# Batch 0 of a two-layer kernel planned anew: x ahead of the mask, the mask in halves, the second bias turned before it is split

## The chip, the cores and the metric

One core of one Trainium2 chip. The metric is the device time of one execution in microseconds, the median of several runs.

## The reference

Eight batches of 256 rows and 1024 features go through two residual layers. In both the identity can be added to the weights.

```python
# layer 1: W0 (o, i), b0, a coefficient for each batch, a mask of 0 and 1 for each batch
x = x + (x @ W0.T + b0 + (x @ (2 * mask[b] - 1)) * coeff[b])
# layer 2: W1 (o, d), b1, and the adapter that ids[b] names (rank 16)
h = x @ A[ids[b]].T
x = x + (x @ W1.T + b1 + h @ B[ids[b]].T)
```

Input and output are float32; x is (8, 256, 1024), the mask (8, 1024, 1024) int32.

## The kernel before

**Precision.** Each float32 operand is split in two float32r parts, hi (a rounding copy, ScalarE) and lo (the rest, VectorE). A product is then three products: hi by hi, lo by hi, hi by lo.

**Tiles.** A chunk n is 128 output features of layer 1 in one batch: n = 8 b + c. make_w (VectorE) makes its weights from the mask and the turned W0, 128x1024; chunk_hi (ScalarE) and chunk_lo (VectorE) split them into whi and wlo. layer1(n, ks) on TensorE takes for each k of 128 inputs one product of 512 columns (whi against x hi and x lo, side by side) and one of 256 (wlo against x hi). The result is y: half_y (ScalarE) adds the bias b0, make_y (VectorE) adds the two halves, y_parts_hi and y_parts_lo split it to yhl. y of chunk c is the c-th input block of layer 2, which sums up in PSUM over the eight chunks. The adapter's h is computed from the same y (adapter_h), and b1 enters as two rows of bt in the closing products.

**Batch 0 against the rest.** From batch 1 on a regular loop runs. In batch 0 all weights have to be brought in and turned too: turn_unit (TensorE) transposes four 128x128 blocks of W0, W1, A, B or x into a PSUM bank; W0, W1, A and B each come in units of four blocks. GpSimd adds the identity to the diagonal block first (eye_w0, eye_w1), ScalarE copies W0 out (copy_w0), ScalarE and VectorE split the others (split_hi, split_lo). For batch 0 the program of every engine and of the DMA queue of SP is a list written out by hand; each engine takes its list in order. Chunks 0 and 1 are made and split in halves (half_make_w, half_chunk_hi, half_chunk_lo), x of batch 0 comes by rows (load_rows) and is turned on TensorE (first_rows_hi, first_rows_lo). x of batch 1 comes by load_x(1) into xraw and is turned on VectorE (turn_rows).

**Start.** SP issues W0 block 0, mask 0, rows 0 of x, b0, rows 1 of x, W0 block 1, mask 1, W1 block 0. TensorE runs products on zeros (idle_products, 512 columns each, in line L1056): five at first, two after the turn of the coefficients, three ahead of chunk 0. first_layer1 takes chunk 0: for k 0 to 3 the whi and the wlo product by turns, then W0's block 1 is turned, then k 4 to 7 in the same way, then the x lo products of k 0 to 7.

**The second bias.** load_b1 brings b1 into one partition (1x1024). bias_parts (GpSimd) makes b1hi and b1lo there; move_bias (SP) moves them to rows 80 and 81 of bt after clear_bt (GpSimd) has cleared bt, which waits for the turns of A. ScalarE's split_hi of B waits for both moves, for b1raw lies in the tile bhl that it writes. SP reads the eight adapter names into registers (read_names) in two groups of four.

**Waits that count below.** first_layer1 waits for x hi (x_hi), for whi and wlo's halves (first_hi, first_lo, w_hi, w_lo) and for x lo (x_lo). layer1(1) waits for first_lo of chunk 1, and its k 4 on for w_lo 2. The turn of W0 block 2 waits for y_made 1, since its bank is the one of chunk 0. first_layer2(c) waits for y_lo and the parts of W1's block c.

Of the kernel before, what the change touches and what calls it, by code (L numbers as in the profile page):

```python
# [7 lines left out]
I32 = mybir.dt.int32  # L8
# [8 lines left out]
def two_layer_kernel(nc, x, coeff, ids, mask, W0, b0, W1, b1, lora_a, lora_b, out):  # L17
# [46 lines left out]
    def parted(u):  # L64

        return sum(v[0] in ("w1", "a", "b") for v in units[:u + 1])

# [53 lines left out]
    with ExitStack() as ctx:  # L121
# [39 lines left out]
        b1raw = nc.alloc_sbuf_tensor_at("b1raw", [1, D], F32, offset=bhl_at)  # L161
        b1lo = nc.alloc_sbuf_tensor_at("b1lo", [1, D], F32R, offset=bhl_at)
        b1hi = nc.alloc_sbuf_tensor_at("b1hi", [1, D], F32R, offset=bhl_at + D * 4)
# [18 lines left out]
        rows_in = [sem(f"rows_in{st}") for st in range(ST)]  # L182
        mask_in = [sem(f"mask_in{s}") for s in range(MS)]
# [60 lines left out]
        def _(sp):  # L244
            def load_mask(n):
                b, c = divmod(n, KT)
                s = n % MS
                if n >= MS:
                    sp.wait_ge(w_lo, n - MS + 1)
                src = mask[b].rearrange("(p k) o -> p k o", k=KT)[:, :, c * P:(c + 1) * P]  # L250
                dst = wm[:, s, :].bitcast(I32).rearrange("p (k o) -> p k o", k=KT)
                sp.dma_start(dst, src).then_inc(mask_in[s], 16)
# [16 lines left out]
            def load_b1():  # L269
                sp.dma_start(b1raw[:, :], b1.rearrange("(e o) -> e o", e=1)).then_inc(b1_in, 16)  # L270
# [28 lines left out]
            def move_bias():  # L299
                sp.wait_ge(consts_set, 3)  # L300
                sp.wait_ge(bias_hi, 1)
                sp.dma_start(bt[80:81, :].bitcast(F32), b1hi[:, :].bitcast(F32)).then_inc(bias_moved, 16)
                sp.wait_ge(bias_lo, 1)
                sp.dma_start(bt[81:82, :].bitcast(F32), b1lo[:, :].bitcast(F32)).then_inc(bias_moved, 16)
# [75 lines left out]
            load_mask(11)  # L380
            load_mask(9)
            load_mask(10)
            load_bt(0)
# [16 lines left out]
        def _(pool):  # L400
# [60 lines left out]
            place_a(1)  # L461
            eye_w1(6)
            eye_w1(7)
            place_a(2)
# [6 lines left out]
        def _(act):  # L471
# [101 lines left out]
            first_rows_hi(0, 0)  # L573
            half_chunk_hi(0, 0)
            first_rows_hi(0, 1)
            first_rows_hi(1, 0)
            half_chunk_hi(0, 1)
            first_rows_hi(1, 1)
            copy_w0(1, 0)
            copy_w0(1, 1)  # L580
            half_y(0)
            half_chunk_hi(1, 0)
            half_chunk_hi(1, 1)
            split_hi("w1", 0, 0)
            split_hi("w1", 0, 1)
            copy_w0(2, 0)
            copy_w0(2, 1)
            y_parts_hi(0)
# [3 lines left out]
            chunk_hi(2)  # L592
            copy_w0(3, 0)
            y_parts_hi(1)
# [8 lines left out]
            copy_w0(4, 1)  # L603
            split_hi("w1", 3, 0)
            y_parts_hi(2)
# [4 lines left out]
            copy_w0(5, 1)  # L610
            split_hi("b", 0, 0)
            chunk_hi(5)
            y_parts_hi(3)
            split_hi("w1", 4, 0)
            split_hi("w1", 4, 1)
            half_y(4)
            copy_w0(6, 0)
            copy_w0(6, 1)
            y_parts_hi(4)
            split_hi("b", 0, 1)  # L620
            split_hi("w1", 5, 0)
            chunk_hi(6)
            half_y(5)
            split_hi("w1", 5, 1)
            copy_w0(7, 0)
            copy_w0(7, 1)
            y_parts_hi(5)
            split_hi("w1", 6, 0)
            chunk_hi(7)
            split_hi("w1", 6, 1)  # L630
            half_y(6)
            rows_hi(1, 1)
            y_parts_hi(6)
            split_hi("w1", 7, 0)
            chunk_hi(8)
            rows_hi(1, 0)
            split_hi("w1", 7, 1)
            half_y(7)
# [30 lines left out]
        def _(dve):  # L669
# [29 lines left out]
            def make_w(n):  # L699
                b, c = divmod(n, KT)  # L700
                dve.wait_ge(mask_in[n % MS], 16 * (n // MS + 1))
# [14 lines left out]
            def half_make_w(n, g):  # L716

                dve.wait_ge(mask_in[n], 16)
# [93 lines left out]
            split_lo("w1", 1, 0)  # L812
            make_y(1)
            split_lo("w1", 1, 1)
# [6 lines left out]
            split_lo("a", 0, 1)  # L821
            chunk_lo(3)
            make_y(2)
            make_w(4)
            split_lo("w1", 3, 0)
            split_lo("w1", 3, 1)
            y_parts_lo(2)
# [419 lines left out]
```

## Time and profile before

| | us |
|---|---|
| median of 3 runs | 407.26 (406.19 to 407.48) |
| the profiled execution | 407.4 |
| its span, first to last instruction | 405.6 |
| TensorE busy | 397.5 (98%) |
| VectorE busy | 293.0 (72%) |
| ScalarE busy | 182.8 (45%) |
| GpSimd busy | 26.7 (7%) |
| DMA, mean | 156 GB/s |

PE is TensorE (PEld its weight loads), DVE VectorE, ACT ScalarE, POOL GpSimd, SP the engine that issues the loads (SPq its DMA issues). A matmul's duration includes its way through the array, so matmuls overlap; from start to start is what one costs in a row. Times are from the start of the span.

### The profile page before, as it was taken

The numbers are of one execution on the slowest core, as the hardware profiler recorded it, in microseconds if no ns is written. First come the engines' busy times: TensorE is split into PE (matmuls) and PEld (weight loads), VectorE is DVE, ScalarE is ACT, GpSimd is POOL, SyncE is SP. The second block draws the span as 40 slices with busy tenths as digits, with TensorE's granted clock in tenths as the row PEclk, the third lists the DMA queues.
The fourth block names the chain that finished last, engine by engine and source line by source line (L and its number), as shares of the span: only waits on it lengthen the run. The fifth ranks groups of instructions, "written<-read, shape, count | busy, mean of one in ns | idle before, by whom it ended". The sixth has DMA issues, their size and how long they took to land.

```text
span 405.6 us, 6148 instructions
## 1 busy us (share of the span) xinstructions
PE 397.5 (98%) x2362; PEld 365.9 (90%) x2362; DVE 293.0 (72%) x375; ACT 182.8 (45%) x289; POOL 26.7 (7%) x43
## 2 busy tenths in 40 slices
PE   7989999999999999999999999999999999999996
PEld 5878888899999999999999999999999999999995
DVE  1797799766977598677887679675987688775523
ACT  2666656443444344343445344354444444353322
POOL 1253121000001000010001000010001000000000
PEclk9999999999999999999999999999999999999999
DMA  8999993659532893159532893249732792346002
GB/s 260 305 251 281 283 231 99 146 156 253 149 103 105 182 221 103 53 152 251 156 105 73 190 228 94 79 127 211 192 104 72 201 242 77 103 133 166 0 2 103
DMA packets 93488, 63.33 MB, mean 156 GB/s; under 512 B 3595, under 2 KB 90643, under 8 KB 93460
## 3 DMA queue, kind: packets, MB, share of 16 engines
q1 hardware_dynamic: 93298, 62.77, 59.7%
q8 instruction: 19, 0.31, 0.3%
q10 hardware_dynamic: 162, 0.18, 0.1%
q14 instruction: 9, 0.07, 0.1%
HBM read 51.39 MB, written 8.39 MB: 147 GB/s over the span
## 4 chain that ended last, share of the span: by engine, by line
PE 95%; DVE 2%; DMA 2%; ACT 0%; SPq 0%; issue 0%
PE ps L951 29%; PE ps L953 15%; PE ps L1022 13%; PE ps L1024 13%; PE ps L1023 13%; PE ps L924 4%; PE ps L1045 2%; PE ps L1000 2%; DMA xrows<-in_x_dram 2%; PE ps L1002 2%; PE ps L1001 2%; DVE yhl L752 1%; PE ps L985 0%; DVE wlo L712 0%; PE ps L1056 0%; DVE h_rows L767 0%
## 5 line engine op out<-in xcount | busy, mean ns | idle before, releaser
L951 PE MATMUL ps<-xhl,whi 128*128 128x512 f32 x504 | 180.3, 396 | 0.0
L953 PE MATMUL ps<-xhl,wlo 128*128 128x256 f32 x504 | 140.9, 280 | 0.0
L951 PEld LDWEIGHTS ps<-xhl,whi 128*128 128x128 f32 x504 | 94.5, 188 | 19.2
L1024 PE MATMUL ps<-w1hi,yhl 128*128 128x344 f32 (+1 forms) x336 | 107.8, 321 | 0.0
L1022 PE MATMUL ps<-w1hi,yhl 128*128 128x344 f32 (+1 forms) x336 | 107.6, 320 | 0.0
L1023 PE MATMUL ps<-w1lo,yhl 128*128 128x344 f32 (+1 forms) x336 | 107.6, 320 | 0.0
L953 PEld LDWEIGHTS ps<-xhl,wlo 128*128 128x128 f32 x504 | 95.0, 189 | 0.5
L712 DVE SCALAR_TENSOR_TENSOR wlo<-wm,cs_minus,whi 128x1024 fp32r<-128x1024 f32 x62 | 79.7, 1285 | 20.6 <-ACT whi L492 20.6
L492 ACT ACTIVATE whi<-wm,cs_minus 128x1024 fp32r<-128x1024 f32 x62 | 71.5, 1153 | 38.1 <-DVE wm L705 38.1
L705 DVE SCALAR_TENSOR_TENSOR wm<-wm,cs_twice,w0t 128x1024 f32<-128x1024 int32 x62 | 79.7, 1286 | 1.1 <-ACT w0t L475 1.1
L748 DVE TENSOR_TENSOR ysum<-ps,ysum 128x256 f32<-128x256 f32 x64 | 27.1, 424 | 59.9 <-ACT ysum L532 59.9
L532 ACT ACTIVATE ysum<-ps,b0col 128x256 f32<-128x256 f32 x64 | 30.3, 473 | 87.4 <-PE ps L953 85.8
L1022 PEld LDWEIGHTS ps<-w1hi,yhl 128*128 128x128 f32 x336 | 63.1, 188 | 3.0 <-DVE yhl L752 0.3
L1023 PEld LDWEIGHTS ps<-w1lo,yhl 128*128 128x128 f32 x336 | 63.2, 188 | 0.0
L1024 PEld LDWEIGHTS ps<-w1hi,yhl 128*128 128x128 f32 x336 | 63.1, 188 | 0.0
L539 ACT ACTIVATE yhl<-ysum 128x256 fp32r<-128x256 f32 x64 | 26.8, 419 | 27.6 <-DVE ysum L748 27.6
L682 DVE STREAM_TRANSPOSE xt<-xraw 128x1024 f32<-128x1024 f32 x14 | 31.2, 2228 | 3.7 <-DMA xraw<-in_x_dram 3.7
L752 DVE TENSOR_TENSOR yhl<-ysum,yhl 128x256 fp32r<-128x256 f32 x64 | 30.0, 469 | 1.2 <-ACT yhl L539 1.2
L517 ACT ACTIVATE xhl<-xt 128x1024 fp32r<-128x1024 f32 x14 | 14.9, 1062 | 21.6 <-DVE xt L682 21.6
L434 POOL CAST w1hi<-at 128x128 fp32r<-128x128 f32 x7 | 6.1, 872 | 223.9 <-PE ps L1024 223.9
L688 DVE TENSOR_TENSOR xhl<-xt,xhl 128x1024 fp32r<-128x1024 f32 x14 | 17.1, 1219 | 0.0
L1000 PE MATMUL ps<-w1hi,yhl 128*128 128x512 f32 x32 | 13.4, 420 | 1.4 <-DVE yhl L752 1.4
(78 smaller groups left out, 241.2 us busy)
## 6 DMA issues: line engine op xcount, KB each, us to landing
wm<-in_mask_Bx4096x_ik_dram SPq DMA_DIRECT2D x64, 512.0 KB, 5.2
xraw<-in_x_dram SPq DMA_DIRECT2D x28, 256.0 KB, 6.3
w0raw<-in_L_cond_W_dram SPq DMA_DIRECT2D x8, 512.0 KB, 6.2
w1raw<-_L_cond_base_weight_dram SPq DMA_DIRECT2D x8, 512.0 KB, 7.3
out_dram<-zst SPq DMA_DIRECT2D x18, 172.0 KB, 2.0
bt<-bhl SPq DMA_DIRECT2D x48, 64.0 KB, 2.4
out_dram<-zst SPq DMA_DIRECT2D x8, 164.0 KB, 2.0
out_dram<-zst SPq DMA_DIRECT2D x7, 176.0 KB, 2.0
```

The costliest lines, as they stand in the source:

```text
L492: nc.scalar.activation(whi[:, n % WS, :, :], wm[:, n % MS, :].rearrange("p (k o) -> p k o", k=KT), ACT.Identity, bias=cs_minus[:, b:b + 1] ...
L532: nc.scalar.activation(ysum[:, n % 2, :], ps[:, l1_bank(n), S:2 * S], ACT.Identity, bias=b0col[:, n % KT:n % KT + 1]).then_inc(y_half, 1)
L682: nc.vector.transpose(xt[:, :, :].rearrange("p t (n q) -> p n t q", q=Q), xraw[:, :, :].rearrange("p n (i k) -> p n k i", k=KT)[:, :, g * ...
L705: nc.vector.scalar_tensor_tensor(chunk, chunk.bitcast(I32), cs_twice[:, b:b + 1], w0t[:, c, :, :].rearrange("p k o -> p (k o)"), ALU.mult, ...
L712: nc.vector.scalar_tensor_tensor(wlo[:, s, :, :], wm[:, n % MS, :].rearrange("p (k o) -> p k o", k=KT), cs_minus[:, b:b + 1], whi[:, s, :, ...
L748: nc.vector.tensor_tensor(row, ps[:, l1_bank(n), 0:S], row, ALU.add).then_inc(y_made, 1)
L752: nc.vector.tensor_tensor(yhl[:, n % 2, S:2 * S], ysum[:, n % 2, :], yhl[:, n % 2, 0:S].bitcast(F32), ALU.subtract).then_inc(y_lo, 1)
L951: nc.tensor.matmul(ps[:, bank, :], whi[:, s, k, :], xhl[:, b % 2, k, :], start=(k == 0), stop=False, skip_group_check=True)
L953: op = nc.tensor.matmul(ps[:, bank, 0:S], wlo[:, s, k, :], xhl[:, b % 2, k, 0:S], start=False, stop=(k == KT - 1), skip_group_check=True)
L1022: nc.tensor.matmul(dst, hi, w1hi[:, c, cols], start=(c == 0), stop=False, skip_group_check=True)
L1023: nc.tensor.matmul(dst, hi, w1lo[:, c, cols], start=False, stop=False, skip_group_check=True)
L1024: op = nc.tensor.matmul(dst, lo, w1hi[:, c, cols], start=False, stop=(c == KT - 1), skip_group_check=True)
```

## The change

No arithmetic is added or left out.

- **Order of the first loads.** W0 block 0, rows 0 of x, b0, the first half of mask 0, rows 1 of x, the second half of mask 0, W0 block 1, mask 1. The mask halves are two DMAs of 256 KB with a semaphore each (first_mask_in), in the same pieces of 512 bytes; half_make_w(0, g) waits for its half.
- **Chunk 0's products in three parts for each half g:** part 0 whi by x hi, part 1 wlo by x hi, part 2 whi by x lo, with a wait of their own each. Order on TensorE: (0,0), (0,1), the turns of W0 block 1, (1,1), (1,0), (0,2), (1,2).
- **Zeros.** Seven at the start, two ahead of the turn of the coefficients (which so comes later), none ahead of chunk 0: nine instead of ten.
- **The second bias.** b1 is loaded as 128x8 (pieces of 32 bytes), split there as 128x8, and the two moves gather the 128 pieces into a row of bt. bias_parts comes after clear_bt and eye_w1(3) on GpSimd; its load comes after that of A's pieces 4 to 7 and mask 3.
- **Batch 0 planned anew** on SP, GpSimd, ScalarE, VectorE and TensorE; the loop from chunk 8 on is as before.

```diff
             load_w0(0)
-            load_mask(0)
             load_rows(0)
             load_b0()
+            load_first_mask(0)
             load_rows(1)
+            load_first_mask(1)
             load_w0(1)
             load_mask(1)
             sp.wait_ge(ids_in, 16)
             load_w1(0)
+            load_w0(2)
             names = read_names(range(0, 4))
-            load_w0(2)
-            load_b1()
-            names += read_names(range(4, 8))
             load_w1(1)
             load_mask(2)
             load_w0(3)
-            load_b(range(0, 2))
+            names += read_names(range(4, 8))
             load_w1(2)
             load_a(range(4, 6))
+            load_a(range(6, 8))
             load_mask(3)
-            load_a(range(6, 8))
+            load_b1()
             load_a(range(0, 2))
             load_a(range(2, 4))
+            load_b(range(0, 2))
             load_w0(4)
             load_w1(3)
             load_mask(4)
+            load_w0(5)
             load_b(range(2, 4))
-            load_w0(5)
-            load_w1(4)
             load_b(range(4, 6))
             load_b(range(6, 8))
+            load_w1(4)
             move_bias()
             load_mask(5)
+            load_w1(5)
             load_w0(6)
             load_w0(7)
             load_mask(6)
-            load_w1(5)
             load_x(1)
...
             load_w1(7)
-            load_mask(11)
+            load_bt(0)
             load_mask(9)
             load_mask(10)
-            load_bt(0)
+            load_mask(11)
```

```diff
+            def load_first_mask(g):
+
+                src = mask[0].rearrange("(p k) o -> p k o", k=KT)[:, g * TG:(g + 1) * TG, 0:P]
+                dst = wm[:, 0, g * HALF:(g + 1) * HALF].bitcast(I32).rearrange("p (k o) -> p k o", k=TG)
+                sp.dma_start(dst, src).then_inc(first_mask_in[g], 16)
...
-                sp.dma_start(b1raw[:, :], b1.rearrange("(e o) -> e o", e=1)).then_inc(b1_in, 16)
+                sp.dma_start(b1raw[:, :], b1.rearrange("(p k) -> p k", k=KT)).then_inc(b1_in, 16)
...
-                sp.dma_start(bt[80:81, :].bitcast(F32), b1hi[:, :].bitcast(F32)).then_inc(bias_moved, 16)
+                sp.dma_start(bt[80:81, :].bitcast(F32).rearrange("e (p k) -> e p k", k=KT), b1hi[:, :].bitcast(F32)).then_inc(bias_moved, 16)
```

GpSimd's and TensorE's lists, the latter to the turns of W0 block 5; ScalarE's and VectorE's follow the same order of chunks.

```diff
             eye_w1(2)
+            eye_w0(4)
+            clear_bt()
+            eye_w1(3)
             bias_parts()
-            eye_w0(4)
-            eye_w1(3)
-            clear_bt()
             eye_w0(5)
             sort_b()
+            place_a(1)
             eye_w1(4)
...
-            idle_products(5)
+            idle_products(7)
             pe.wait_ge(ident_set, 2)
             turn_unit("w0", 0, 0)
             turn_unit("w0", 0, 1)
-            pe.wait_ge(coeff_spread, 1)
-            nc.tensor.transpose(ps[:, L1B, 0:NB], cs_rows[:, :], ident[0:NB, 0:NB]).then_inc(coeff_turned, 1)
             idle_products(2)
+            turn_coeff()
             turn_unit("x", 0, 0)
             turn_unit("x", 0, 1)
-            turn_b0()
             turn_unit("x", 1, 0)
             turn_unit("x", 1, 1)
-            idle_products(3)
-            first_layer1(range(0, 4), False)
+            turn_b0()
+            first_layer1(0, 0)
+            first_layer1(0, 1)
             turn_unit("w0", 1, 0)
             turn_unit("w0", 1, 1)
-            first_layer1(range(4, 8), False)
-            first_layer1(range(0, 4), True)
-            first_layer1(range(4, 8), True)
+            first_layer1(1, 1)
+            first_layer1(1, 0)
+            first_layer1(0, 2)
+            first_layer1(1, 2)
             turn_unit("w1", 0, 0)
             turn_unit("w1", 0, 1)
+            layer1(1, range(0, 2))
             turn_unit("w0", 2, 0)
+            layer1(1, range(2, 4))
             turn_unit("w0", 2, 1)
-            layer1(1, range(0, 2))
-            layer1(1, range(2, 4))
             layer1(1, range(4, 6))
             turn_unit("w1", 1, 0)
             turn_unit("w1", 1, 1)
             layer1(1, range(6, 8))
             first_layer2(0, 0, 0)
+            first_layer2(0, 1, 0)
             first_layer2(0, 0, 1)
             turn_unit("w0", 3, 0)
-            first_layer2(0, 1, 0)
+            first_layer2(0, 1, 1)
             turn_unit("w0", 3, 1)
-            first_layer2(0, 1, 1)
             turn_unit("w1", 2, 0)
+            layer1(2, range(0, 2))
             turn_unit("w1", 2, 1)
+            layer1(2, range(2, 4))
+            layer1(2, range(4, 6))
+            turn_unit("a", 0, 0)
+            turn_unit("a", 0, 1)
+            layer1(2, range(6, 8))
             first_layer2(1, 0, 0)
             first_layer2(1, 1, 0)
-            layer1(2, range(0, 2))
-            turn_unit("a", 0, 0)
-            turn_unit("a", 0, 1)
             first_layer2(1, 0, 1)
-            layer1(2, range(2, 4))
-            layer1(2, range(4, 6))
-            layer1(2, range(6, 8))
             turn_unit("w0", 4, 0)
-            adapter_h(0)
             turn_unit("w0", 4, 1)
             first_layer2(1, 1, 1)
+            adapter_h(0)
+            adapter_h(1)
             turn_unit("w1", 3, 0)
             turn_unit("w1", 3, 1)
             layer1(3, range(0, 2))
             layer1(3, range(2, 4))
             layer1(3, range(4, 6))
             turn_unit("w0", 5, 0)
+            adapter_h(2)
             layer1(3, range(6, 8))
             turn_unit("w0", 5, 1)
```

VectorE's list of chunk 0 and 1:

```diff
             half_make_w(0, 0)
+            first_rows_lo(0, 0)
             half_make_w(0, 1)
-            first_rows_lo(0, 0)
             half_chunk_lo(0, 0)
             first_rows_lo(1, 0)
             half_chunk_lo(0, 1)
+            move_b0()
             first_rows_lo(0, 1)
-            move_b0()
             first_rows_lo(1, 1)
             half_make_w(1, 0)
             half_make_w(1, 1)
+            half_chunk_lo(1, 0)
             make_y(0)
-            half_chunk_lo(1, 0)
+            split_lo("w1", 0, 0)
             half_chunk_lo(1, 1)
-            split_lo("w1", 0, 0)
+            y_parts_lo(0)
             split_lo("w1", 0, 1)
-            y_parts_lo(0)
             make_w(2)
```

## Rows read from the trace of the kernel before

**Rows 1.** Page, part 1: busy time and share of each engine.

```profile
PE 397.5 (98%) x2362; PEld 365.9 (90%) x2362; DVE 293.0 (72%) x375; ACT 182.8 (45%) x289; POOL 26.7 (7%) x43
```

**Rows 2.** Stretches: from:to length, busy of each engine, granted clock, DMA share, GB/s.

```profile
23.30:29.50 6.20, 4.80 (x30) 3.96 (x28) 6.16 (x7) 4.31 (x8) 4.66 (x3) 1.00 1.05 227
29.50:80.60 51.10, 51.05 (x293) 43.96 (x294) 42.36 (x49) 29.47 (x48) 9.98 (x15) 1.00 0.84 212
80.60:405.60 325.00, 321.31 (x1935) 300.89 (x1933) 232.17 (x301) 137.25 (x213) 6.91 (x11) 1.00 0.53 137
```

**Rows 3.** Waits, whole span: who <- for whom: us, times, longest.

```profile
PE ps L1000 <- DVE yhl L752: 1.4, 1, 1.4
...
PEld ps L924 <- DVE ysum L748: 0.4, 1, 0.4
```

**Rows 4.** Timeline to 20 us, TensorE: start, duration, line, op [idle before].

```profile
1.32 2.50 PE L1056 MATMUL ps<-zeros 128*128 128x512 f32 x5 [1.32 <-POOL zeros L437]
...
4.96 1.94 PE L924 MATMUL ps<-ident,w0raw 128*128 128x128 f32 x8 [1.14 <-POOL w0raw L405]
...
8.60 1.97 PE L924 MATMUL ps<-ident,xrows 128*128 128x128 f32 x8 [0.34 <-DMA xrows<-in_x_dram]
...
12.33 1.50 PE L1056 MATMUL ps<-zeros 128*128 128x512 f32 x3
...
13.67 0.28 PE L973 MATMUL ps<-xhl,whi 128*128 128x256 f32 x1
...
17.44 1.04 PE L924 MATMUL ps<-ident,w1raw 128*128 128x128 f32 x8
...
18.63 1.16 PE L924 MATMUL ps<-ident,w0raw 128*128 128x128 f32 x8
...
19.57 0.50 PE L951 MATMUL ps<-xhl,whi 128*128 128x512 f32 x1
```

**Rows 5.** Timeline to 20 us, ScalarE and VectorE.

```profile
9.82 0.60 ACT L522 ACTIVATE xhl<-ps 128x512 fp32r<-128x512 f32 x1 [2.28 <-PE ps L924]
...
10.32 0.71 ACT L502 ACTIVATE whi<-wm,cs_minus 128x512 fp32r<-128x512 f32 x1
...
15.97 1.62 DVE L721 SCALAR_TENSOR_TENSOR wm<-wm,cs_twice,w0t 128x512 f32<-128x512 int32 x2 [0.85 <-ACT w0t L475]
```

**Rows 6.** Timeline: the split of the second bias, and yhl's low part twice.

```profile
25.88 3.22 POOL L416 TENSOR_TENSOR b1lo<-b1raw,b1hi 1x1024 fp32r<-1x1024 f32 x1
...
26.81 2.58 DVE L752 TENSOR_TENSOR yhl<-ysum,yhl 128x256 fp32r<-128x256 f32 x1
...
47.04 0.41 DVE L752 TENSOR_TENSOR yhl<-ysum,yhl 128x256 fp32r<-128x256 f32 x1
```

**Rows 7.** Landings of mask 0, A's last, x(1)'s last piece; starts of users.

```profile
DMA to landing us min/median/max: 5.5/5.5/5.5
...
L292 SPq DMA_DIRECT2D araw<-in_L_cond_lora_A_w_dram x1: 315/315/315, 25.2 to 25.2; - x1
...
DMA to landing us min/median/max: 5.2/5.2/5.2
...
31.72 1.04 PE L924 MATMUL ps<-ident,araw 128*128 128x128 f32 x8
...
33.80 0.46 POOL L410 TENSOR_TENSOR w1raw<-w1raw,ident 128x128 f32<-128x128 f32 x1 [1.33 <-DMA w1raw<-_L_cond_base_weight_dram]
...
37.20 1.03 PE L924 MATMUL ps<-ident,w1raw 128*128 128x128 f32 x8
...
L261 SPq DMA_DIRECT2D xraw<-in_x_dram x1: 1113/1113/1113, 45.4 to 45.4; - x1
...
DMA to landing us min/median/max: 9.6/9.6/9.6
...
57.42 2.24 DVE L682 STREAM_TRANSPOSE xt<-xraw 128x1024 f32<-128x1024 f32 x1
...
67.36 0.48 PE L951 MATMUL ps<-xhl,whi 128*128 128x512 f32 x1
```

More of the change, by code:

```diff
@@ L182, in two_layer_kernel @@
         rows_in = [sem(f"rows_in{st}") for st in range(ST)]
+        first_mask_in = [sem(f"first_mask_in{g}") for g in range(2)]
         mask_in = [sem(f"mask_in{s}") for s in range(MS)]
@@ L460, in _ @@
             eye_w1(5)
-            place_a(1)
+            place_a(2)
             eye_w1(6)
             eye_w1(7)
-            place_a(2)
             pool.wait_ge(z_done, sums_before(1))
@@ L821, in _ @@
             split_lo("a", 0, 1)
+            make_y(2)
             chunk_lo(3)
-            make_y(2)
             make_w(4)
             split_lo("w1", 3, 0)
+            y_parts_lo(2)
             split_lo("w1", 3, 1)
-            y_parts_lo(2)
             chunk_lo(4)
@@ L834, in _ @@
             split_lo("w1", 4, 1)
+            chunk_lo(5)
             make_y(4)
-            chunk_lo(5)
             make_w(6)
-            y_parts_lo(4)
             split_lo("b", 0, 1)
             split_lo("w1", 5, 0)
+            y_parts_lo(4)
             chunk_lo(6)
+            split_lo("w1", 5, 1)
             make_y(5)
-            split_lo("w1", 5, 1)
             turn_rows(1, 1)
+            y_parts_lo(5)
             make_w(7)
-            y_parts_lo(5)
+            rows_lo(1, 1)
             split_lo("w1", 6, 0)
+            chunk_lo(7)
+            make_y(6)
+            split_lo("w1", 6, 1)
             make_w(8)
-            split_lo("w1", 6, 1)
-            make_y(6)
-            chunk_lo(7)
-            rows_lo(1, 1)
             y_parts_lo(6)
@@ L956, in layer1, with first_layer1 @@
                     op.then_inc(l1_done, 1)
-            def first_layer1(ks, low):
-                if ks[0] == 0 and not low:
-                    pe.wait_ge(first_lo, 1)
-                for k in ks:
-                    if k == TG and not low:
-                        pe.wait_ge(w_lo, 1)
-                    if k % TG == 0 and low:
-                        pe.wait_ge(x_lo, first_lo_split(ST - 1, k // TG))
-                    elif k % TG == 0:
-                        pe.wait_ge(x_hi, first_split(ST - 1, k // TG))
-                    if low:
-                        op = nc.tensor.matmul(ps[:, l1_bank(0), S:], whi[:, 0, k, :], xhl[:, 0, k, S:],
-                                              start=(k == 0), stop=(k == KT - 1), skip_group_check=True)
-                    else:
-                        nc.tensor.matmul(ps[:, l1_bank(0), 0:S], whi[:, 0, k, :], xhl[:, 0, k, 0:S],
-                                         start=(k == 0), stop=False, skip_group_check=True)
-                        nc.tensor.matmul(ps[:, l1_bank(0), 0:S], wlo[:, 0, k, :], xhl[:, 0, k, 0:S],
-                                         start=False, stop=(k == KT - 1), skip_group_check=True)
-                if low and ks[-1] == KT - 1:
+            def first_layer1(g, part):
+                if part == 0 and g == 0:
+                    pe.wait_ge(first_hi, 1)
+                elif part == 0:
+                    pe.wait_ge(w_hi, 1)
+                elif part == 1 and g == 0:
+                    pe.wait_ge(first_lo, 1)
+                elif part == 1:
+                    pe.wait_ge(w_lo, 1)
+                if part == 2:
+                    pe.wait_ge(x_lo, first_lo_split(ST - 1, g))
+                else:
+                    pe.wait_ge(x_hi, first_split(ST - 1, g))
+                weights = wlo if part == 1 else whi
+                cols = slice(S, 2 * S) if part == 2 else slice(0, S)
+                for k in range(g * TG, (g + 1) * TG):
+                    op = nc.tensor.matmul(ps[:, l1_bank(0), cols], weights[:, 0, k, :], xhl[:, 0, k, cols],
+                                          start=(k == 0 and part != 1), stop=(k == KT - 1 and part > 0), skip_group_check=True)
+                if g == 1 and part == 2:
                     op.then_inc(l1_done, 1)
@@ L1051, in turn_b0, with turn_coeff @@
                 nc.tensor.transpose(ps[:, L1B, 0:KT], b0row[:, :], ident[0:KT, 0:KT]).then_inc(b0_turned, 1)
+            def turn_coeff():
+                pe.wait_ge(coeff_spread, 1)
+                nc.tensor.transpose(ps[:, L1B, 0:NB], cs_rows[:, :], ident[0:NB, 0:NB]).then_inc(coeff_turned, 1)
             def idle_products(count):
@@ L1126, in _ @@
             first_layer2(2, 1, 0)
             layer1(4, range(4, 6))
+            turn_unit("w1", 4, 1)
+            first_layer2(2, 1, 1)
             layer1(4, range(6, 8))
[L1129 removed]
             turn_unit("w0", 6, 0)
+            adapter_h(3)
             turn_unit("w0", 6, 1)
             first_layer2(3, 0, 0)
[L1133 removed]
+            first_layer2(3, 1, 0)
             turn_unit("b", 0, 1)
[L1135 removed]
+            layer1(5, range(0, 2))
```

88 lines of the change are left out of this document (43 added, 45 removed).

## The prediction

> **What bounds the kernel now.** I read the page's shares first: TensorE is busy 397.5 of 405.6 us [rows 1], so time can only come from its work, its waits, or its speed. The stretches say where the 8 us without it lie: from 80.6 us on it is busy 321.3 of 325.0, from 29.5 to 80.6 it is busy 51.05 of 51.10, and from 23.3 to 29.5 only 4.80 of 6.20 [rows 2]. The list of waits names the largest one after the start: 1.4 us for VectorE's yhl, the low part of y of chunk 1, then 0.4 us for ysum [rows 3]. The timeline of the first 20 us gives the rest: 1.3 us before the first instruction, 1.1 us before the first transposes (while GpSimd adds ident to w0(0)), 0.3 us for x, and fillers (the products on zeros) that count as busy but do nothing for the output: five at 1.32, three at 12.33 [rows 4].
>
> The same rows show a second loss that no share shows. Eight transposes take 1.97 us at 8.60 and 1.04 us at 17.44; three fillers of 512 columns take 1.50 us at 12.33, as much as 1.2 GHz needs, while the products of chunk 0 start at 13.67 at the rate of 2.4 GHz [rows 4]. The granted clock reads 1.00 throughout [rows 2], so here it is the durations that tell the level: lower until about 13.6 us, upper afterwards. From 30 us on the kernel is a full queue on TensorE. Hence the sum: whatever makes TensorE reach its state at 30 us earlier is kept to the end, if no other engine or load becomes late.
>
> **Part 1: x ahead of the mask, mask in halves, products in three parts.** Now rows 0 of x land at 8.60 (TensorE waits for them), after chunk 0's mask, issued at 1.2 and landed 5.5 later, at 6.7 [rows 4, 7]. Both are 512 KB, so in the new order x should land at about 6.7, the first half of the mask 0.9 later (half of the 1.9 between the two landings), at 7.6, rows 1 near 9.2 and the second half near 10. Bounds for a half: nothing later than the whole mask's place in the present queue, and 2 us later if two issues cost more than one.
> TensorE: the transposes of w0(0) still wait for GpSimd and start at 4.96; the seven fillers end before (two more are 0.9 us, beside a wait of 1.1). Then come two fillers (0.9) and the turn of the coefficients, which is put behind them, so x starts at 7.75 instead of 8.60. x(0) takes 1.9 at the lower level, x(1) starts at about 9.6.
> ScalarE: its first x part comes 1.2 us after the transposes start (9.82 against 8.60) [rows 4, 5], so now at 9.0. Four x parts of 0.6 and the half of whi of 0.7 [rows 5], at the pace at which the units arrive, put the third x part's end at 11.6. VectorE has the first half of wlo ready at 11.8 (0.8, as one of the two halves of w that take 1.62 [rows 5]).
> So the first products start at 11.7 instead of 13.67. Four products of 256 columns are 0.85 us at the lower level and 0.47 at the upper: the first two parts fill 11.7 to 13.4, w0(1)'s eight transposes 13.4 to 14.2 (0.8 start to start), two more parts go to 15.3. The part with wlo's second half needs 13.5 on VectorE, and does not wait. The last part needs x's last low part, VectorE 14.9. It ends at 16.2, against 17.44 when the w1 transposes begin behind it [rows 4]: 1.2 us.
> What is late next is VectorE. It makes w of chunk 1 from 14.9 instead of 15.97, where today it waits for the w0 copy [rows 5]. Two halves of 0.8 and wlo's half, again near 0.75, give 17.2. TensorE has done w1(0)'s transposes at 17.0, so it waits 0.2. Today it starts chunk 1 at 19.57, behind w0(2)'s transposes of 18.63 [rows 4], which wait 0.4 for ysum [rows 3]; in the new order w0(2) comes inside chunk 1. The like place is therefore 18.63, and the shift there is 1.4. The second half of wlo(1) is ready at about 19.55, when TensorE arrives at 19.6: an even race. Splitting w0(2) costs one or two restarts of 0.1. I carry a shift of 1.25 through chunk 1, bounds 0.6 (VectorE 0.6 late at the even race) and 1.7 (no wait, clock up earlier).
>
> **Part 2: the second bias.** Today GpSimd splits it as 1x1024: 3.22 us from 25.88, and beside it VectorE's yhl takes 2.58 us instead of 0.41 [rows 6]; TensorE's 1.4 us wait ends with exactly that instruction [rows 3, 6]. As 128x8 the two steps work on 8 elements of a partition. The trace has no such step on GpSimd; above it is bounded by the 0.46 us of a 128x128 step [rows 7], below by nothing. I take 0.2 each. Without the stall yhl would end 2.2 us earlier, before TensorE asks, and its order is changed too (chunk 2 of layer 1 goes ahead of layer 2 of chunk 1), so the whole 1.4 goes; what is late next is wlo of chunk 2, about 25 on VectorE against 26 on TensorE. The step also moves behind clear_bt and w1(3). SP stands in move_bias until it is done, with mask 5, w1(5), w0(6), w0(7), mask 6 and x(1) queued behind in SP's program. It arrives there near 35, and w1(3) is added to ident on GpSimd at 33.80 today [rows 7], so the bias is split by 34.7: no new wait, up to 1 us on SP if w1(3) lands late. The moves and the load are now 128 pieces of 32 bytes. Nothing in the trace prices these; ScalarE needs them only for the first b unit.
>
> **Part 3: the new plan of batch 0.** No TensorE work is added or removed but one filler (nine instead of ten) and a few restarts; there is nothing to gain where TensorE is busy 51.05 of 51.10 [rows 2], so it can only lose. The loads set this. The DMA engines are full from 23.3 to 29.5 (share 1.05) and at 0.84 over the next 51 us [rows 2], so the loads do not come earlier, while TensorE comes 2.6 us earlier. Adapter a: the last piece is issued at 25.2 and lands at 30.4, TensorE turns it at 31.72 [rows 7], and would now, 2.65 us earlier with seven pieces of layers 1 and 2 behind chunk 1 as before, want it at about 29.0. It gets ahead of b and the bias, issued some 1.6 us earlier, landing at 28.8: I charge 0.2, bounds 0 and 1.3. w1(3): turned at 37.20 today [rows 7], 2.65 earlier and behind one adapter product more it is wanted at about 34.8; it is ready at 34.3 (33.80 + 0.46), behind the same bytes: 0 to 0.5. x(1): the last piece lands at 45.4 + 9.6 = 55.0, VectorE turns it at 57.42 [rows 7], and now wants it at 54.8; VectorE may stand 0.2 to 0.5, with y_parts_lo(5), make_w(7) and chunk_lo(7) queued behind it. chunk_lo(7) ends some 6.7 us after that turn begins (2.24 for the turn, the other steps 4.5 by their kind), and TensorE, which takes chunk 7 of layer 1 at 67.36 today [rows 7], wants it at about 64.8: three us of cover. load_bt(0) goes ahead of masks 9 to 11; six small issues, in a stretch with slack. place_a(1) is put ahead of w1(4) on GpSimd; w1(4) then has about 1 us of cover left.
>
> **Sum.** 1.25 + 1.4 - 0.2 for a, +0.1 for the filler and small waits = 2.55 us. The profiled execution took 407.4 us with a span of 405.6, so 1.8 lie outside it; it becomes 403.05 + 1.8 = 404.85. It stands 0.14 above the median of the runs, 407.26, so the forecast is 404.7.
>
> **Rivals.**
> (a) One gain is swallowed: VectorE or the landing of a, w1(3) or b takes about half. For it: the even race at 19.6 and three covers under 1 us. Against it: VectorE loses 2.2 us of stall at 27, and TensorE's order puts long pieces of layer 1 ahead of what was late. Lower ends of the parts, 0.6 + 1.4 - 0.8: 1.2 us, so about 406.0.
> (b) The clock, which ends on the slower side. Place: 11 to 20 us. Today three fillers, 1.5 us without a pause, stand just ahead of the rise at 13.6 [rows 4]; they are gone. Price: each us for which the lower level lasts longer costs 0.5 us of TensorE, less what VectorE covers. If the rise comes at 17, at the end of chunk 0's products, 1.4 us are lost: 406.2. The forecast's gain is used up when the lower level lasts until 18.8, and the kernel is slower by over 0.3% (1.2 us more) from a rise at 21.2, say 408.8. Against it: the fillers are replaced by real products at 11.7, as long as the fillers were, and TensorE has fewer pauses ahead of them.
> The Trainium skill speaks for this rival: "TensorE: Matmul & The Clock Gate", Part 4: PE-mode transpose, says that transposes do not count as TensorE activity for the clock as products do. By that rule the x transposes do nothing for the clock and the removed fillers did; the trace agrees as far as 16 transposes of x from 8.60 to 12.3 ran wholly at the lower level, and the rise came only after fillers, but it does not tell the one cause from the other.
> (c) More is gained: the rise comes ahead of the x(1) transposes, the race at 19.6 is won, and a lands in time: 1.7 + 1.4 + 0.1 = 3.2, so 404.1, or a little less, 403.9.
>
> **How the numbers follow.** Forecast 0.50 (404.0 to 405.5); (a) 0.22; (b) 0.13 near 406.2 and 0.07 slower; (c) 0.08. A measurement of this kernel can tell about 0.3% from no change, which is 1.2 us: faster ends at 406.0, slower begins at 408.5. The forecast and (c) are faster whole, (a) for half, (b) for a quarter of its 0.13: 0.50 + 0.08 + 0.11 + 0.03, 0.72; same 0.11 of (a) and 0.10 of (b), 0.21; slower 0.07. The range leaves out the slow end of (b) and the best of (c): 403.6 to 406.6.
>
> **What would show it.** Right, step by step: x's transposes start near 7.8; the first product of chunk 0 at 11.7 and the w1 transposes behind the last one at 16.2 to 16.6; chunk 1 near 17.3; transposes at 0.1 us each from 13.6 at the latest; GpSimd's bias steps under 0.5 us and no yhl over 0.6 us; no TensorE wait over 0.3 us between 20 and 80; the last product of batch 0 2.5 us earlier than now. Wrong: a TensorE wait on a, w1(3) or wlo(1) (a), products of 256 columns at 0.21 us apart after 14 us (b), or a hole on VectorE at x(1) that reaches TensorE.

## The result

The changed kernel takes 404.77 us, the median of 7 runs (404.1 to 406.26), against 407.26 before (406.17 to 409.27): ratio 0.9946, interval 0.9925 to 0.9968. The forecast was 404.7. A second set of runs, on another chip, gave 0.9966 (0.9946 to 0.9987). So it is faster by 1.4 to 2.2 us. The profiled execution, 406.26 us with a span of 404.5, is the longest of the seven: what follows explains an execution 1.5 us slower than the median, whose span is only 1.1 us shorter than that of the trace of before.

Page of the changed kernel, parts 1 to 3 (busy, packets):

```profile
PE 394.7 (98%) x2361; PEld 363.7 (90%) x2361; DVE 288.9 (71%) x375; ACT 183.5 (45%) x289; POOL 21.5 (5%) x43
...
DMA packets 93870, 63.33 MB, mean 157 GB/s; under 512 B 3978, under 2 KB 91026, under 8 KB 93842
```

The same bytes and, but for one filler, the same products; TensorE's busy time is 2.8 us less than in [rows 1], VectorE's 4.1 and GpSimd's 5.2. Timeline of the changed kernel, TensorE:

```profile
1.33 3.35 PE L1075 MATMUL ps<-zeros 128*128 128x512 f32 x7 [1.33 <-POOL zeros L449]
4.78 1.38 PE L939 MATMUL ps<-ident,w0raw 128*128 128x128 f32 x8
...
6.71 1.16 PE L939 MATMUL ps<-ident,xrows 128*128 128x128 f32 x8
...
8.35 1.16 PE L939 MATMUL ps<-ident,xrows 128*128 128x128 f32 x8 [0.48 <-DMA xrows<-in_x_dram]
...
9.85 0.71 PE L990 MATMUL ps<-xhl,whi 128*128 128x256 f32 x4 [0.19 <-ACT xhl L534]
...
14.84 1.07 PE L939 MATMUL ps<-ident,w1raw 128*128 128x128 f32 x8 [0.70 <-POOL w1raw L422]
...
15.66 0.48 PE L966 MATMUL ps<-xhl,whi 128*128 128x512 f32 x1
...
29.34 0.84 PE L939 MATMUL ps<-ident,araw 128*128 128x128 f32 x6 [1.51 <-DMA araw<-in_L_cond_lora_A_w_dram]
...
79.31 0.39 PE L1051 MATMUL ps<-bt,ht 128*128 128x512 f32 x1
```

Against [rows 4]: eight x transposes take 1.16 us instead of 1.97, chunk 0's products start at 9.85 instead of 13.67, chunk 1 at 15.66 instead of 19.57 (3.0 earlier than the like place, 18.63). A is turned at 29.34 against 31.72 [rows 7]: of 3.0 us in hand, and the wait of 1.4 us for yhl gone as well, 2.4 are left. At the closing product of batch 0 (80.50 in the first trace of before) 1.2 are left. From there to the end it is 325.2 us in the changed kernel (404.5 less 79.31) and 325.1 in the one before (405.6 less 80.50). So all of the change, gain and loss, lies ahead of 80 us, and in this execution more than half of what the head (all that lies ahead of chunk 1) gained was given back by then. TensorE's waits say where:

```profile
PE ps L939 <- DMA araw<-in_L_cond_lora_A_w_dram: 1.5, 1, 1.5
...
PE ps L939 <- POOL w1raw L422: 1.2, 2, 0.7
PE ps L939 <- DVE bhl L687: 1.2, 1, 1.2
PE ps L939 <- DMA xrows<-in_x_dram: 0.5, 1, 0.5
```

The wait for yhl of [rows 3] is gone; in its place stand A, W1's blocks (0.7 ahead of chunk 1, 0.5 at 24.65), and bhl, the split of B. That last one is a load too, one step removed. VectorE stood for mask 6 with B's split queued behind it in its list (timeline of the changed kernel, VectorE):

```profile
51.28 1.28 DVE L717 SCALAR_TENSOR_TENSOR wm<-wm,cs_twice,w0t 128x1024 f32<-128x1024 int32 x1 [2.43 <-DMA wm<-in_mask_Bx4096x_ik_dram]
52.48 1.08 DVE L687 TENSOR_TENSOR bhl<-ps,bhl 128x512 fp32r<-128x512 f32 x1
```

Mask 6 was issued at 39.1 and landed 12.1 us later. The DMA engines are full all the while (stretches of the changed kernel, as in [rows 2]):

```profile
20.00:27.50 7.50, 6.98 (x43) 6.04 (x42) 4.49 (x8) 4.67 (x8) 0.92 (x2) 1.00 1.14 219
...
30.00:52.00 22.00, 22.00 (x137) 19.36 (x136) 14.19 (x18) 14.85 (x24) 8.63 (x15) 1.00 1.12 279
```

The DMA share is over 1 in both, but the bytes are not at one rate, 219 and 279 GB/s.

### The profile page after: what moved, and what is told of

It is laid out like the page before. It is cut to its first block, busy times and chain, and to the rows that moved or that the text cites. A ratio compares the mean times of both kernels' runs of the same rounds, so it can differ in the third digit from the quotient of the medians.

```text
span 404.5 us, 6149 instructions
## 1 busy us (share of the span) xinstructions
PE 394.7 (98%) x2361; PEld 363.7 (90%) x2361; DVE 288.9 (71%) x375; ACT 183.5 (45%) x289; POOL 21.5 (5%) x43
## 4 chain that ended last, share of the span: by engine, by line
PE 87%; SPq 5%; DMA 4%; DVE 2%; issue 1%; ACT 0%
PE ps L966 27%; PE ps L968 14%; PE ps L1037 13%; PE ps L1039 13%; PE ps L1038 13%; DMA wm<-in_mask_Bx4096x_ik_dram 3%; PE ps L1060 2%; DMA araw<-in_L_cond_lora_A_w_dram 1%; PE ps L939 1%; SPq L287 1%; PE ps L1017 1%; PE ps L1015 1%; PE ps L1016 1%; SPq L298 1%; SPq L303 1%
## 5 line engine op out<-in xcount | busy, mean ns | idle before, releaser
L551 ACT ACTIVATE yhl<-ysum 128x256 fp32r<-128x256 f32 x64 | 26.8, 419 | 27.9 <-DVE ysum L763 27.5
L767 DVE TENSOR_TENSOR yhl<-ysum,yhl 128x256 fp32r<-128x256 f32 x64 | 27.5, 429 | 1.0 <-ACT yhl L551 1.0
L529 ACT ACTIVATE xhl<-xt 128x1024 fp32r<-128x1024 f32 x14 | 14.9, 1064 | 20.1 <-DVE xt L694 20.1
L687 DVE TENSOR_TENSOR w1lo<-ps,w1hi 128x512 fp32r<-128x512 f32 x16 | 10.8, 687 | 5.0 <-ACT w1hi L497 4.9
```

What stands on the lines that cost most here:

```text
L767: nc.vector.tensor_tensor(yhl[:, n % 2, S:2 * S], ysum[:, n % 2, :], yhl[:, n % 2, 0:S].bitcast(F32), ALU.subtract).then_inc(y_lo, 1)
```

## The experiments

Two theories. **Loads:** the loads keep the DMA engines full until about 52 us and do not come earlier, so whatever lets TensorE arrive earlier is given back at the next load. **Sum:** the parts add up. Beside them stood a question on the clock: do the seven fillers bring the upper level early, or is it chance? Every kernel was timed against the kernel before on the same chip; the ratios are to that one. There were four sets, on which the kernel before had these medians: 407.26 with the changed kernel (after); 406.88 with b_narrow, a_wide, a_fill5 and b_fill7; 406.59 with b_head, a_mask_first and a_again; 406.51 with a_early, a_mask6, a_both and both_mask_first. Medians of different sets are therefore compared by their ratios.

| kernel | x | chunk 0 | chunk 1 | A | closing | median us | ratio (95%) |
|---|---|---|---|---|---|---|---|
| before | 8.60 | 13.67 | 19.57 | 31.72 | 80.50 | 407.26 | |
| b_again | 8.70 | 13.15 | 19.05 | 30.09 | 79.53 | | |
| b_fill7 | 8.62 | 13.78 | 19.90 | 32.12 | 80.95 | 406.32 | 0.9988 (0.9968, 1.0008) |
| b_narrow | 8.32 | 11.87 | 17.82 | 32.12 | 81.00 | 406.26 | 0.9983 (0.9963, 1.0002) |
| b_head | 6.49 | 10.06 | 17.33 | 29.78 | 79.21 | 406.04 | 0.9980 (0.9963, 0.9997) |
| after | 6.71 | 9.85 | 15.66 | 29.34 | 79.31 | 404.77 | 0.9946 (0.9925, 0.9968) |
| a_again | 6.50 | 10.35 | 16.20 | 29.14 | 78.12 | 405.08 | 0.9966 (0.9946, 0.9987) |
| a_fill5 | 7.59 | 10.73 | 16.05 | 28.67 | 77.48 | 404.88 | 0.9952 (0.9932, 0.9972) |
| a_mask_first | 7.94 | 11.08 | 16.67 | 29.32 | 79.72 | 405.53 | 0.9980 (0.9961, 0.9999) |
| a_wide | 6.39 | 9.75 | 15.60 | 28.45 | 79.68 | 406.59 | 1.0001 (0.9974, 1.0028) |
| a_early | 6.81 | 9.95 | 15.74 | 28.31 | 78.34 | 404.78 | 0.9956 (0.9937, 0.9975) |
| a_mask6 | 6.67 | 9.87 | 15.94 | 29.50 | 78.77 | 405.74 | 0.9982 (0.9964, 1.0000) |
| a_both | 6.55 | 9.76 | 15.83 | 28.07 | 79.94 | 405.26 | 0.9966 (0.9948, 0.9984) |
| both_mask_first | 8.98 | 12.36 | 17.79 | 29.12 | 78.66 | 405.74 | 0.9977 (0.9951, 1.0003) |

The columns x to closing are starts on TensorE in the one trace of each kernel, from its timeline: the first transposes of x, the first products of chunk 0 and of chunk 1, the transposes of A, the first closing product. Executions of one kernel differ by more than most of these kernels do (the changed one took 403.58 to 406.97 us over both sets, the one before 404.71 to 409.73), so a single trace shows which waits there are, not what they cost in the median.

### The second bias, alone and undone

b_narrow is the kernel before with these lines of the change and no other; a_wide is the changed kernel with them undone:

```diff
-        b1raw = nc.alloc_sbuf_tensor_at("b1raw", [1, D], F32, offset=bhl_at)
-        b1lo = nc.alloc_sbuf_tensor_at("b1lo", [1, D], F32R, offset=bhl_at)
-        b1hi = nc.alloc_sbuf_tensor_at("b1hi", [1, D], F32R, offset=bhl_at + D * 4)
+        b1raw = nc.alloc_sbuf_tensor_at("b1raw", [P, KT], F32, offset=bhl_at)
+        b1hi = nc.alloc_sbuf_tensor_at("b1hi", [P, KT], F32R, offset=bhl_at + KT * 4)
+        b1lo = nc.alloc_sbuf_tensor_at("b1lo", [P, KT], F32R, offset=bhl_at + 2 * KT * 4)
```

> The kernel before with the second bias as 128x8 (load, split, moves) and nothing else. Both theories: the 1.4 us wait of TensorE for yhl at 29.5 us goes, GpSimd's two bias steps take under 1.5 us together instead of 4.3, no yhl step on VectorE is over 0.7 us. If the parts of the change simply add up, the time is 1.4 us lower than the kernel before (ratio about 0.9966). If the loads are the next bound, TensorE comes 1.4 us earlier to the transposes of A, whose last piece lands 1.3 us before TensorE wants it today, so 1.2 to 1.4 us are still gained.

> The changed kernel with the second bias as 1x1024 again (load, split, moves), all orders as in the changed kernel. If the parts add up: slower than the changed kernel by 1.4 us or more, since GpSimd's 4 us stall VectorE again. If loads bind the changed kernel up to 54 us (its trace shows TensorE standing 1.5 us for A and 1.2 us behind a late mask): the stall falls on time that is idle anyway, the time is within 0.6 us of the changed kernel.

b_narrow's ratio is 0.7 us lower, half of what was expected, with an interval from 1.5 us lower to 0.1 higher, so that no gain at all is not ruled out. The bias steps are short (0.44 and 0.21 us), no yhl stalls, but TensorE now waits for W0's block 3:

```profile
PE ps L924 <- POOL w0raw L405: 3.1, 2, 2.0
```

(The other 1.1 us is the wait at the start.) That block was issued at 14.6 and landed 9.4 us later; in the trace of before it was issued at 14.9 and landed 6.7 later. So the load itself came 2.3 us later here. Whether that is scatter or the 128 small pieces of b1, issued 3.7 us ahead of it, was not tried.

The pause has a second price in this trace. Its stretches from 20 us on (length, busy, then granted clock, DMA share, GB/s at the end):

```profile
20.00:24.00 4.00, 3.14 (x20) 2.44 (x18) 3.63 (x6) 2.60 (x4) 0.00 (x0) 1.00 0.98 257
24.00:27.00 3.00, 1.86 (x11) 1.76 (x12) 0.88 (x2) 0.90 (x2) 1.46 (x3) 0.90 0.75 188
27.00:31.00 4.00, 4.00 (x18) 3.42 (x17) 1.05 (x3) 1.79 (x3) 0.48 (x2) 0.65 0.86 263
```

The clock is granted 0.90 and 0.65 of full behind the pause of 2.0 us, 1.2 GHz for a part of each. The head start that this trace had at chunk 1 (17.82 against 19.57) was gone at A (32.12, later than before).

a_wide costs 1.4 to 2.2 us against the changed kernel (1.0001 against 0.9966 and 0.9946). In its own set stands a_fill5, the changed kernel but for two fillers, with 0.9952 (0.9932 to 0.9972) against 0.9974 to 1.0028 for a_wide, so the loads did not hide it. In its place behind W1's block 3 the wide step falls on w of chunk 4 (timeline of a_wide, GpSimd, VectorE, TensorE):

```profile
33.03 3.24 POOL L428 TENSOR_TENSOR b1lo<-b1raw,b1hi 1x1024 fp32r<-1x1024 f32 x1
...
33.97 4.78 DVE L717 SCALAR_TENSOR_TENSOR wm<-wm,cs_twice,w0t 128x1024 f32<-128x1024 int32 x1
...
36.24 0.45 POOL L417 TENSOR_TENSOR w0raw<-w0raw,ident 128x128 f32<-128x128 f32 x1
...
36.64 1.03 POOL L436 COPY bsort<-braw 128x1024 f32<-128x1024 f32 x1
...
39.41 0.72 PE L939 MATMUL ps<-ident,w0raw 128*128 128x128 f32 x4 [2.07 <-DVE w1lo L687]
```

VectorE's step ended only at 38.75, 2.5 us after the bias step: two more steps of GpSimd, the last two of its rows shown, ran beside it with no gap (in the changed kernel they start at 35.73 and 37.30, apart). So here the loads theory was wrong and the sum nearer: the stall comes behind A's wait, with its own place on VectorE.

### The fillers and the clock

a_fill5 is the changed kernel with idle_products(5) for idle_products(7), b_fill7 the kernel before with 7 for 5; b_again is the kernel before once more, a_again the changed one.

> The changed kernel with five fillers at the start instead of seven. Theory clock: the two more fillers are what brings the upper level before w0(0)'s transposes end; with five, x's transposes take 0.21 us each, the products of chunk 0 start 1 to 2 us later than 9.85, and as the loads bind later stretches the time rises by 0 to 0.8 us only. Rival: the early rise comes from the order of x or by chance; then x's transposes stay at 0.1 us each and nothing changes.

> The kernel before with seven fillers at the start instead of five, nothing else. Theory clock: the upper level comes before 8.6 us, x's transposes take 0.1 us each, and chunk 0's products start 0.8 to 1.5 us earlier than 13.67, the time falls by 0.7 to 1.5 us. Rival: x's transposes stay at 0.21 us, the rise stays near 13.5 us and the time is the same within 0.3 us.

> The kernel before unchanged, for a second trace. If the moment of the rise is the program's doing, it is near 13.5 us again, behind the three fillers. If it is free, it lies elsewhere (the kernel with seven fillers at the start had it near 14.3, the one with the narrow bias near 9.4).

> The changed kernel unchanged, for a second trace and more times. If the moment at which the clock rises is the program's doing, x's transposes take 0.1 us each again and the rise is near 5.4 us. If it is free, it lies elsewhere between 4 and 9 us, and the waits for A and for W1's block 5 (1.5 and 1.2 us in the first trace) shift by as much as TensorE comes later.

Neither experiment on the fillers shows an effect on the time: a_fill5 0.9952 beside 0.9946 and 0.9966 for the changed kernel, b_fill7 0.9988 with 1 in its interval. Timeline of b_fill7, then of b_head, which run the same TensorE program up to the end of W0's first transposes:

```profile
1.32 3.35 PE L1056 MATMUL ps<-zeros 128*128 128x512 f32 x7 [1.32 <-POOL zeros L437]
4.81 1.94 PE L924 MATMUL ps<-ident,w0raw 128*128 128x128 f32 x8
```

```profile
1.32 3.35 PE L1075 MATMUL ps<-zeros 128*128 128x512 f32 x7 [1.32 <-POOL zeros L449]
4.81 1.13 PE L939 MATMUL ps<-ident,w0raw 128*128 128x128 f32 x8
```

The same work with the same starts: 1.94 us at the lower level in the one, 1.13 at the upper in the other. The moment of the rise is not the program's alone. Yet it is not all chance either: in the four traces with the old head the x transposes begin at the lower level, in the eight with x first at the upper one, with five fillers too (a_fill5: sixteen in 2.03 us). What in the new head does it the runs do not tell, but they narrow it down. It is not the order of the loads: in a_mask_first and both_mask_first the mask comes ahead of x again, and x's transposes still begin at the upper level (at 7.94 and 8.98). It is not the number of fillers, by a_fill5 and b_fill7. And it is not pauses ahead of x: a_fill5 stands 0.88 us ahead of W0's transposes and is at the upper level by 7.59, b_fill7 has no pause up to 8.10 and stays at the lower one until about 14. Nor does it take the three fillers of the old head, behind which the rise came in the trace of before: in b_narrow, with the same program on TensorE, it came at about 9.4, amid x's transposes and ahead of the three fillers:

```profile
8.32 1.57 PE L924 MATMUL ps<-ident,xrows 128*128 128x128 f32 x8
...
9.98 1.16 PE L924 MATMUL ps<-ident,xrows 128*128 128x128 f32 x8
```

b_again had no wait for yhl at all: the bias step fell there on w of chunk 3 (1.90 us on VectorE), and TensorE waited 0.4 for A instead. Its one execution took 407.21 us, within the range of the other runs of this kernel.

### The head alone, and undone

b_head is the kernel before with the new order of the first six loads, the mask halves, the three parts, the fillers and the lists of chunk 0. a_mask_first is the changed kernel with this:

```diff
+            load_first_mask(0)
+            load_first_mask(1)
             load_rows(0)
             load_b0()
-            load_first_mask(0)
             load_rows(1)
-            load_first_mask(1)
```

> The kernel before with the new head only: x ahead of the mask, the mask in halves, chunk 0 in three parts, seven and two fillers, the lists of chunk 0 as in the changed kernel; the second bias wide and the plan behind chunk 0 as before. If the sum of the prediction holds, chunk 0's products end 1.2 us earlier at the same clock, the 1.4 us wait for yhl stays, and the time falls by 1.2 to 1.4 us (ratio about 0.997). If the head's gain in the changed kernel was the early clock alone, the time is within 0.5 us of before and depends on when the transposes change from 0.21 to 0.1 us each.

> The changed kernel with both halves of mask 0 loaded ahead of x, all else as changed. If the order of x carries the head's gain: x lands near 8.6 us again, chunk 0's products start 1.3 to 2 us later than 9.85, and the time rises by 0.8 to 1.5 us. If the loads of A, W1 and the masks bind later anyway, the late head is absorbed by those waits and the time stays within 0.5 us of the changed kernel.

b_head gains 0.8 us (0.1 to 1.5), less than the 1.2 to 1.4 expected, though its products start 3.6 us earlier. Its waits:

```profile
PE ps L939 <- POOL w1raw L422: 2.6, 3, 1.5
...
PE ps L939 <- DMA araw<-in_L_cond_lora_A_w_dram: 0.2, 1, 0.2
```

W1's block 2 is late now, 1.5 us. The 1.4 us wait for yhl, which was expected to stay since the second bias is still wide, is not in the list: as in b_again the wide step fell on w of chunk 3 (1.89 us). By the ratios the head alone and the bias alone gain 0.8 and 0.7 us, 1.5 together; the whole change gains 1.4 in one set and 2.2 in the other. So in the final time the parts do add up within the noise, each at less than was expected of it, and the noise is too large to say whether the rest of the plan adds anything. a_mask_first starts chunk 1 1.0 us later than the changed kernel and turns A at 29.32 against 29.34: the wait for A shrank from 1.5 to 1.0, the rest went in others. Its median is 0.5 us above that of the changed kernel in the same set (by the ratios 0.6 and 1.4 us above the two sets), and the intervals overlap; whether x first is worth anything in the final time was not settled.

### Taking the loads' waits away

a_early loads A's pieces 0 to 3 ahead of mask 3 and b1, a_mask6 loads mask 6 ahead of W0's block 7, a_both does both, both_mask_first adds the edit of a_mask_first.

```diff
             load_a(range(6, 8))
+            load_a(range(0, 2))
+            load_a(range(2, 4))
             load_mask(3)
             load_b1()
-            load_a(range(0, 2))
-            load_a(range(2, 4))
...
             load_w0(6)
-            load_w0(7)
             load_mask(6)
+            load_w0(7)
```

> The changed kernel with all eight pieces of A loaded ahead of mask 3 and b1. If A's landing pins TensorE at about 29 us (it turns A at 28.5 to 29.8 in six traces whose chunk 1 starts anywhere from 15.6 to 17.3), the wait for A of 1.0 to 1.5 us shrinks below 0.4 and A is turned near 28; mask 3 lands 0.8 us later, which VectorE has cover for. Time 0.5 to 1.2 us lower than the changed kernel. Rival, the queue only changes place: the wait moves to mask 3 or W1 block 3 and the time is the same within 0.3 us.

> The changed kernel with mask 6 loaded ahead of W0's block 7. If the 1.2 us wait of TensorE at 52.4 us comes from mask 6 (VectorE stood 2.4 us for it with B's split queued behind), VectorE's wait falls under 1 us, TensorE's under 0.2, and the time falls by up to 1.2 us where the wait occurs; the second trace of the changed kernel had only 0.2 there, so 0.3 to 0.8 us in the median. Rival: the wait is chance, time the same within 0.3 us.

> Both of these. If both waits are the loads' and independent: 1.0 to 1.8 us lower than the changed kernel, ratio to the kernel before 0.990 to 0.993. If taking away one exposes the other (the loads as a whole are the bound until 54 us), no more than the better of the two alone.

> As a_both, with both halves of mask 0 loaded ahead of x. With the changed plan alone this made chunk 1 start 1.0 us later and A was turned at the same moment. If A's landing no longer pins TensorE, the later head now shows: 0.5 to 1.0 us slower than a_both. If the loads still bind, within 0.3 us of a_both.

Each wait that was aimed at goes, and another one stays or grows. In a_early no wait for A is listed and A is turned at 28.31; the waits are now these:

```profile
PE ps L939 <- POOL w1raw L422: 1.7, 2, 1.1
...
PE ps L939 <- DVE bhl L687: 1.1, 1, 1.1
```

Its ratio of 0.9956 lies between the two sets of the changed kernel: the gain of 0.5 to 1.2 us did not come. In a_mask6 VectorE makes w of chunk 6 at 49.11 without a wait, the one for bhl is not in the list, and A's is 1.9. Its ratio of 0.9982 is 0.7 and 1.5 us above the changed kernel's, where 0.3 to 0.8 lower or the same were expected; why, one trace does not show. In a_both W1's blocks take what A and mask 6 gave back:

```profile
PE ps L939 <- POOL w1raw L422: 2.5, 2, 1.8
...
PE ps L939 <- DVE bhl L687: 1.2, 1, 1.2
```

and its bhl wait comes 8.7 us earlier than in the changed kernel, behind mask 5 (timeline of a_both, VectorE):

```profile
42.60 1.28 DVE L717 SCALAR_TENSOR_TENSOR wm<-wm,cs_twice,w0t 128x1024 f32<-128x1024 int32 x1 [3.36 <-DMA wm<-in_mask_Bx4096x_ik_dram]
```

None of the four is faster than the changed kernel beyond its interval. Of the expectations the last of a_both's held, no more than the better of the two alone, which fits that the loads as a whole are the bound. In the traces both_mask_first is the plainest witness. It starts chunk 1 2.0 us later than a_both, has no wait for A, bhl or a late block over 0.6 us, and closes batch 0 at 78.66 against 79.94. In all nine traces with the changed plan the closing product lies between 77.48 and 79.94, whatever the start of chunk 1 (15.60 to 17.79). By the ratios both_mask_first is 0.4 us above a_both, with intervals that overlap, so its two expectations (0.5 to 1.0 slower, or within 0.3) cannot be told apart. That the loads bind is thus read from the waits; the runs changed only the order of the loads, none their number or size. Its late head is partly the clock's, which fell behind a pause of 1.5 us for x (stretches):

```profile
4.80:6.90 2.10, 2.06 (x10) 2.05 (x10) 0.00 (x0) 0.68 (x2) 0.00 (x0) 1.00 1.01 250
7.20:10.20 3.00, 1.40 (x10) 1.10 (x9) 0.99 (x3) 0.61 (x2) 0.00 (x0) 0.99 1.00 388
10.20:13.60 3.40, 3.35 (x15) 2.99 (x16) 2.91 (x5) 3.01 (x6) 0.46 (x1) 0.50 1.17 324
```

## Why the prediction was right, and where it was not

The time was right, 404.7 against 404.77, and so was the sign. That the two agree to 0.1 us is luck: the kernel before had a median of 407.26 in that set and 406.5 to 406.9 in the three others, and by the ratios the gain is 2.2 us in one set and 1.4 in the other, not 2.55. The sum was made of terms that were wrong in both directions. What follows measures them in the profiled execution, the slowest of the seven, so in the median the losses must have been smaller or the gains larger. The trace of a_again (405.08 us, the median of its set) has waits of 1.0 us for A, 0.3 for W1's block 2 and 0.2 for bhl in the places of the 1.5, 0.5 and 1.2 below, and closes batch 0 at 78.12, 2.4 us ahead of the first trace of before.

- **The head, 1.25 us.** Measured 3.0 us at the like place in the profiled execution. The order of events was right; what failed is the clock, which was carried at the lower level until 13.6 us from the one trace of before. x started at 6.71 instead of 7.75, took 1.16 instead of 1.9, and ScalarE's parts came accordingly. Rows 1 of x landed at 8.35, earlier than the 9.2 expected. In the time, the head alone was worth 0.8 us (b_head), not 1.25.
- **VectorE at chunk 1.** The race at 19.6 us was not the limit; TensorE waited 0.7 us for W1's block 0, which GpSimd had only at 14.08, when the load landed. This load was never asked for in the prediction, since TensorE was expected after it.
- **The bias, 1.4 us.** The mechanism was right and the size was one trace's. b_narrow gave 0.7 us (1.5 to -0.1); of the four traces with the wide bias and the old plan behind chunk 0, before and b_fill7 have the wait for yhl (1.4 and 1.5), b_again and b_head do not. In the changed plan the wide step cost more, 1.4 to 2.2 us (a_wide). The bound for a 128x8 step was wrong as well; one took 1.20 us (timeline of the changed kernel, GpSimd):

```profile
32.98 1.20 POOL L426 CAST b1hi<-b1raw 128x8 fp32r<-128x8 f32 x1
34.27 0.20 POOL L428 TENSOR_TENSOR b1lo<-b1raw,b1hi 128x8 fp32r<-128x8 f32 x1
```

  It began 0.1 us after VectorE's wlo of 1.28 us; that it waited for that step is likely and was not tried.
- **The loads, -0.2 us.** Measured -3.2: 1.5 for A, 1.2 for bhl behind mask 6, 0.5 for another block of W1. A's landing was forecast well (28.8; the last piece was issued at 23.2 and landed 6.0 later, at 29.2). The term that was mis-sized is the wait for it, 0.2 where it measured 1.5. What was wrong is when TensorE would ask: 27.8, not 29.0, because the head had gained more. Mask 6 was not checked at all; it was one of the loads queued behind move_bias.
- **Net.** In this execution 3.0 + 1.4 - 3.2 = 1.2 us at the closing product, as measured. The excess of the head and part of the excess of the waits belong together: TensorE came to A 1.2 us before the 29.0 expected, and A's wait was longer by 1.3. The 1.2 us behind mask 6 were no such return but a term left at nothing. Rival (a), a gain swallowed by the landing of a, and the early rise of rival (c) both came, each against the other.
- **Rival (b), the clock.** Did not happen. The rise does not need the three fillers: in the new head it came without them, before x, and in b_narrow, whose TensorE program is that of before, it came ahead of them. The Trainium skill's sentence that transposes do not count as TensorE activity for the clock as products do ("TensorE: Matmul & The Clock Gate", Part 4: PE-mode transpose) is not refuted: b_fill7 stayed at the lower level through 16 transposes of x (8.62 to 12.35), as the trace of before did. But as it was used here, against the removal of three fillers, it pointed the wrong way: the rise came earlier, with seven fillers at the start and with five, and in b_narrow amid x's transposes.

## What to carry to other kernels

Where loads keep the DMA engines full, list for each of them the moment of landing and the moment of use before an edit moves the user earlier; what is won beyond the cover (the time from landing to use) can return as a wait on a load, on the compute engine or, one step removed, on the engine that prepares its data with other work queued behind. A wait read from one trace is one sample: the 1.4 us that a long GpSimd step cost TensorE was 0.7 in the median and nothing in the next trace, and one load landed 2.3 us later in one trace than in another. A step on one partition that stretches another engine's steps is worth spreading over all partitions even so; at another place of the plan it cost 1.4 to 2.2 us.

## What the runs showed of the hardware

- The same TensorE program with the same starts ran at the lower level in one execution (eight transposes in 1.94 us, b_fill7) and at the upper in another (1.13, b_head). With one TensorE program the level rose at about 13.6 us in one execution (before) and at about 9.4 in another (b_narrow).
- A pause of 1.5 to 2.0 us was followed by a stretch with the granted clock at half: 0.50 from 10.2 to 13.6 us in both_mask_first, 0.90 and 0.65 from 24 to 31 us in b_narrow. Pauses of 1.5 us (at A in the changed kernel), 1.9 (in a_mask6) and 2.07 us (in a_wide) were not.
- A VectorE step that takes 1.28 us elsewhere took 4.78 in a_wide, beside a GpSimd step of 3.24 us on one partition and two more behind it (0.45 and 1.03); one of 0.41 us took 2.58 beside a GpSimd step of 3.22 [rows 6].
- With the DMA share over 1, loads moved 219 GB/s in one stretch and 279 in another (changed kernel, 20 to 27.5 and 30 to 52 us).
